# A decoder layer on one core: the last job's inverse sums spread by TensorE, VectorE's steps reordered, maxima in two operations per block

## The reference, cut to what matters

```python
# x (4, 1024, 256), 16 heads of 16; ctx (4, 77, 256)
x = x + attn(layernorm(x))            # windowed causal self attention, chunks of 128, each with the chunk before
x = x + xattn(layernorm(x), ctx, ctx) # cross attention on 77 keys with a mask
x = x + ffn(layernorm(x))             # fake-quantised gated feed-forward, 704 wide
...
def xattn(...):
    attn = softmax(scores)            # per head and token
    out = einsum('bhqk,bhkd->bhqd', attn, v)
    return out @ Wo.T + bo
...
def ffn(x, ...):
    xq = act_fake_quant(x, clip_x)    # scale = sigmoid(clip) * max|x| / 127 over the WHOLE tensor
    h = act_fake_quant(silu(xq @ Wg.T) * (xq @ Wu.T), clip_down)   # again one scale from max|h| over everything
    return h @ Wd.T                   # weights fake-quantised per row
```

## Time and profile before

| | us |
|---|---|
| median of 3 runs | 696.22 |
| lowest and highest | 692.82, 696.35 |
| profiled execution, time | 694.38 |
| its span, first to last instruction | 692.5 |
| busy: TensorE, VectorE, ScalarE, GpSimd | 606.5, 513.6, 406.5, 165.0 |
| passage, last value product to the first quantised x | 552 to 582 |
| up phase | 587 to 651 |
| down phase, to the end | 655 to 692.5 |

### The profile page before, as it was taken

How to read it: one execution, slowest core, us unless ns; L and a number is a source line. 1 busy time by engine, 2 the same in 40 slices (tenths; PEclk the granted TensorE clock), 3 DMA queues, 4 the chain that set the end, 5 groups by cost and what they waited for, 6 DMA issues and landing times.

```text
span 692.5 us, 19989 instructions
## 1 busy us (share of the span) xinstructions
PE 606.5 (88%) x8020; PEld 394.3 (57%) x8020; DVE 513.6 (74%) x986; ACT 406.5 (59%) x602; POOL 165.0 (24%) x213
## 2 busy tenths in 40 slices
PE   2799999999998999999999999999979843887395
PEld 2567575767764766576757655567546532333173
DVE  6698777777787586757866866686697466799787
ACT  3346666665675548556564576444545714999692
POOL 2014333322343302320441133220120001455200
PEclk9899999999999999999999999999999966999789
DMA  7744233552353344256324353443474320000024
GB/s 255 189 152 132 58 119 98 153 147 77 99 144 102 109 114 103 70 147 158 113 73 128 90 131 103 112 121 85 99 212 102 76 48 1 0 1 1 0 92 153
DMA packets 58554, 72.17 MB, mean 104 GB/s; under 512 B 23979, under 2 KB 35423, under 8 KB 58463
## 3 DMA queue, kind: packets, MB, share of 16 engines
q1 hardware_dynamic: 54783, 68.92, 35.9%
q10 hardware_dynamic: 3680, 1.97, 1.1%
HBM read 17.74 MB, written 4.72 MB: 32 GB/s over the span
## 4 chain that ended last, share of the span: by engine, by line
PE 57%; DVE 14%; SPq 10%; DMA 6%; issue 6%; ACT 4%; POOL 0%; ACTq 0%; DVEq 0%; POOLq 0%
PE banks L483 37%; PE banks L663 7%; SPq L416 5%; PE banks L583 4%; PE banks L674 3%; DVE mtop L1100 3%; SPq L434 2%; SPq L411 2%; PE banks L527 2%; DVE tops L1283 2%; PE banks L728 1%; DVE big L1277 1%; DMA oTs<-oe 1%; DVE parts L1265 1%; DMA big<-parts 1%
## 5 line engine op out<-in xcount | busy, mean ns | idle before, releaser
L483 PE MATMUL banks<-big 96*128 96x77 bf16 (+3 forms) x1344 | 157.6, 238 | 9.3 <-DMA big<-kparts 2.9
L1100 DVE TENSOR_REDUCE mtop<-banks 128x4 f32<-128x640 f32 (+3 forms) x128 | 127.2, 1020 | 40.6 <-PE banks L592 39.8
L483 PEld LDWEIGHTS banks<-big 99*128 99x128 bf16 (+2 forms) x1344 | 102.2, 101 | 75.7 <-issue 34.8
L899 ACT ACTIVATE big<-banks 128x1024 f32<-128x1024 f32 x96 | 97.0, 1028 | 38.3 <-PE banks L483 38.0
L1380 POOL TENSOR_SCALAR_AFFINE_SELECT big<-big 128x512 f32<-128x512 f32 x96 | 64.5, 672 | 229.8 <-ACT big L899 228.9
L483 PE MATMUL banks<-xnT,weights 128*128 128x512 f32 x192 | 91.6, 606 | 0.1
L583 PE MATMUL banks<-big 96*32 96x160 bf16 (+3 forms) x1792 | 71.3, 259 | 0.5 <-DVE mtop L1100 0.2
L903 ACT ACTIVATE big<-banks 77x1024 f32<-77x1024 f32 x48 | 47.9, 1021 | 27.4 <-PE banks L483 25.4
L1104 DVE TENSOR_REDUCE mtop<-banks 128x8 f32<-128x616 f32 x64 | 49.3, 790 | 17.5 <-PE banks L483 17.2
L663 PE MATMUL banks<-big 128*17 128x256 f32 x768 | 57.0, 382 | 0.0
L912 ACT COPY oe<-banks 128x512 f32<-128x512 f32 x64 | 36.7, 588 | 33.6 <-DMA oTx<-oe 10.7
(11 more groups left out here) (160 smaller groups left out, 1187.0 us busy)
## 6 DMA issues: line engine op xcount, KB each, us to landing
big<-parts SPq DMA_DIRECT2D x285, 128.0 KB, 2.4
oc<-sums SPq DMA_DIRECT2D x16, 512.0 KB, 4.7
oTs<-oe SPq DMA_DIRECT2D x64, 64.0 KB, 2.5
...
```

The costliest lines, as they stand in the source:

```text
L483: return e.matmul(to[0:w], k[:, 0:w], q, start=start, stop=stop, skip_group_check=True)
L899: e.activation(pt[u].rearrange("p (i n) -> p i n", i=4)[:, :, 0:n], pair(p).rearrange("p j (s n) -> p (j s) n", s=2)[:, :, 0:n], ACT.Exp, ...
L1100: e.tensor_reduce(M.rearrange("p (h c) -> p h c", h=4)[:, :, c], pair(p).rearrange("p j (s n) -> p (j s) n", s=2)[:, :, 0:160 + 32 * (c % 4)],
```

## The change

Four things change.

- The last job's inverse sums (x31) don't go through DRAM. Its store and widen are gone. GpSimd builds a 128x128 matrix of ones and zeros (`heads`: row p has ones in the 16 columns of its head) in the step pick, in the middle of the kernel, and VectorE a 128x16 one (`group`). In the new steps broad, VectorE multiplies the 128x64 reciprocals by `group` into a 128x512 operand for each half of the tokens, and TensorE multiplies it by `heads`, which gives each partition its head's inverse sums, in a PSUM bank. The scaling of x31 reads that bank in place of `oc`. The two new bank holders shift the banks of the four last out steps and of the last wturn.
- On VectorE, the steps stat3 2 5, 2 6 and 2 7, top3 2 4 and 2 6, root3 2, and wtile 1 4, 1 5, 2 0 and 2 1 stand ahead of the last invert. Before, they stood between it and the scaling of x31, or behind that (wtile 2 1). Then follow invert x31, broad 0, broad 1, scale x30, scale x31 and end3 2. On SyncE, the spreads of x31's second group stand directly behind its gather.
- On TensorE the two broad products stand between the wturn 2 0 and the first out step of x3.
- In the up phase the tops of a block are two operations of three tiles, put behind tiles 1 and 4 of the next block, in place of three of two tiles behind tiles 0, 2 and 5. Block 7 keeps three of two tiles. So there are 17 maxima in place of 24.

```diff
--- before.py
+++ after.py
@@ -27,6 +27,7 @@
 JOBS = [(j[0].lower(), int(j[1]), "ab".index(j[2]))
         for j in "S0a S0b S1a S1b S2a X0a S2b X0b S3a X1a S3b X1b X2a X2b X3a X3b".split()]
 AT = {j: n for n, j in enumerate(JOBS)}
+LAST_SELF = [j for j in JOBS if j[0] == "s"][-1]
 UNITS = {"s": NC, "x": 4}
 HALF_AT = {"s": 3, "x": 1}
 
@@ -41,9 +42,9 @@
     "sgvmrTqpsvmtvexmvmqsccosmdosmvmemvsmssvhvrmmtwomsnipvsmvemhmgsqnhscvrqhmmAqsvnvsCogeccxsvqvnBvtcpsou"
     "rsVosvDMuedpVMtsvmnvegnvmsyknosmysvvmmsmemivmwsnRrqNvecqmAvBocptsvmmsmvmssmmveesTyNmrvvsgTysvsyitqqs"
     "veCskxdvvssvmwmvycgsemspvACcsmvgvpsmvstsvveBrkyhmvvmemxsysgsrsdptvimvmmwuvemevrqqCgYussAsmvsmvxvmccd"
-    "vtehmeoonnonipsnrsonnhntsnBsRwhvmmmveANvgpCmgNBssTsevTrxqqccpodwtomoUgosmyvvuvvemmkeshysprtys1svmykv"
-    "gimmquysvsveesmhrCcsvvutveuvAhdmxyqesycs2mysmYmpsvvhwitgvrveh22km3B4mmsmxses4r44v4o45t4oy4o5y5osp4mv"
-    "554memmeryiUuvvu5styysspsiv5yeyxuvvye5Y5vg5sssseue44vU4vvxvd455p5ogyyowgjyyojdypyojyyJYjJJJ6E5w")
+    "vtehmeoonnonipsnrsonnhntsnBsRwhvmmmveANvgpCmgNBssTsevTrxqqccpodwtomoUgosmyvvuvvemmkeshysprtysP1svmyk"
+    "vgimmquysvsveesmhrCcsvvutveuvAhdmxyqesycs2mysmYmpsvvhwitgvrveh22km3B4mmsmxses4r44v4o45t4oy4o5y5osp4m"
+    "v554memmeryiUuvvu5styysspsv5yeyuvvye5Y5vg5sssseue44v4vvvd455p5ibbxxUogyyowgjyyojypyojyyJYjJJJ6E5")
 
 
 def root_of(kind, b, c):
@@ -70,8 +71,10 @@
         "g": [("gather", job, g) for job, g in turns],
         "p": [("spread", job, g) for job, g in turns],
         "i": [("invert", job) for job in JOBS],
-        "d": [("store", job) for job in JOBS],
-        "w": [("widen", job) for job in JOBS],
+        "d": [("store", job) for job in JOBS[:-1]],
+        "w": [("widen", job) for job in JOBS[:-1]],
+        "b": [("broad", half) for half in range(2)],
+        "P": [("pick",)],
         "x": [("scale", job) for job in JOBS],
         "o": [("out",) + layer + (c,) for layer in layers for c in range(0, NC, 2)],
         "n": [("stats",) + layer + (c,) for layer in layers for c in range(NC)],
@@ -130,7 +133,7 @@
 
 
 WIDE = {"turned": 2, "max": 2, "score": 2, "up": 2}
-NARROW = {"turnw", "turnc", "masks", "keys", "qk", "v", "xkeys", "turnm", "out", "wturn", "turnx", "down", "dsc", "peak"}
+NARROW = {"turnw", "turnc", "masks", "keys", "qk", "v", "xkeys", "turnm", "out", "broad", "wturn", "turnx", "down", "dsc", "peak"}
 
 
 def banks_of(steps, count_of):
@@ -217,6 +220,9 @@
         winv = sb("winv", [128, 16], F32)
         banks = ctx.enter_context(nc.psum_tensor("banks", [128, 8, 512], F32))
         acc = banks[:, 6:8, :]
+        heads = big[:, 21888:22016]
+        group = big[:, 22016:22032]
+        grown = rem.rearrange("p i n -> p (i n)")
         r_dram = nc.dram_tensor("sums", [8, S], F32, kind="Internal").ap()
 
         x_dram = x_in.rearrange("b (c p) d -> p (b c) d", p=128)
...
@@ -317,6 +324,8 @@
                 return a_xnT, 2 * n
             if k == "wturn":
                 return a_wT, w_done(s)
+            if k == "broad":
+                return d_scale, len(JOBS) + s[1]
             return {"turnw": a_turnw, "turnc": d_ctx, "masks": d_mask, "keys": a_keys, "qk": d_rem, "v": a_v,
                     "xkeys": d_xv, "max": d_max, "turnm": a_m3t, "score": a_exp, "out": d_out}[k], {
                         "turnw": 2 * n, "masks": 2 * n, "keys": 3 * n - 2, "xkeys": 2 * n}.get(k, n)
@@ -685,6 +694,10 @@
                             t = whole(bank(p)[:, i * 256:i * 256 + 256], oT[kind][f][:, (c + i) * 128:(c + i) * 128 + 128],
                                        wo[:, f, :] if kind == "s" else xw[:, 3, f, :], i == 0 and f == 0, f == 1)
                     t.then_inc(t_out, 1)
+                elif k == "broad":
+                    e.wait_ge(p_pick, 3)
+                    e.wait_ge(d_broad, s[1] + 1)
+                    whole(bank(p), heads, grown[:, s[1] * 512:s[1] * 512 + 512], True, True).then_inc(t_broad, 1)
                 elif k == "wturn":
                     _, z, t0 = s
                     e.wait_ge(a_wb, n_of["wtile", z, t0])
@@ -775,11 +788,11 @@
                 if blk < 6 and t in (1, 3):
                     ffn += [("narrow", blk + 2, t - 1), ("narrow", blk + 2, t)]
                 ffn.append(("hid", blk, t))
-                if blk and t in (0, 2, 5):
-                    ffn.append(("top", blk - 1, t // 2 * 2))
+                if blk and t in (1, 4):
+                    ffn.append(("top", blk - 1, 0 if t == 1 else 3, 3))
                 if blk == 7 and t in (3, 5):
-                    ffn.append(("top", 7, t - 3))
-        ffn += [("top", 7, 4), ("scaleh",), ("peak", 1), ("quanth", 0), ("dsc",)]
+                    ffn.append(("top", 7, t - 3, 2))
+        ffn += [("top", 7, 4, 2), ("scaleh",), ("peak", 1), ("quanth", 0), ("dsc",)]
         for blk in range(8):
             if blk < 7:
                 ffn.append(("quanth", blk + 1))
@@ -1124,16 +1137,37 @@
                     if n:
                         e.wait_ge(land_r, 32 * n - 16)
                     e.reciprocal(ls[:, 1, :], ls[:, 0, :]).then_inc(d_inv, 1)
+                elif k == "pick":
+                    e.wait_ge(p_set, 2)
+                    e.wait_ge(t_val, n_of[end_val(LAST_SELF, 1)])
+                    e.tensor_reduce(group, ident.rearrange("p (h j) -> p j h", h=8), AX.X, ALU.max).then_inc(d_pick, 1)
+                elif k == "broad":
+                    e.wait_ge(d_inv, len(JOBS))
+                    if s[1] == 0:
+                        e.wait_ge(d_pick, 1)
+                        e.wait_ge(a_p1, n_of["split", JOBS[-1], 0, 1])
+                        e.wait_ge(d_p2, n_of["split", JOBS[-1], 0, 1])
+                    e.tensor_tensor(grown[:, s[1] * 512:s[1] * 512 + 512].rearrange("p (j n) -> p j n", j=8),
+                                    ls[:, 1, :].rearrange("p (a n) -> p a n", a=1).to_broadcast([128, 8, 64]),
+                                    group[:, 8 * s[1]:8 * s[1] + 8].rearrange("p (j a) -> p j a", a=1
+                                                                              ).to_broadcast([128, 8, 64]),
+                                    ALU.mult).then_inc(d_broad, 1)
                 elif k == "scale":
                     job = s[1]
                     kind, b, f = job
                     n = AT[job]
-                    e.wait_ge(land_r, 32 * (n + 1))
+                    last = n == len(JOBS) - 1
+                    if not last:
+                        e.wait_ge(land_r, 32 * (n + 1))
                     for g in range(2):
                         e.wait_ge(land_o[g], 64 * (n + 1))
-                    cuts = (0, 512, S) if n == len(JOBS) - 1 else (0, S)
-                    for a, z in zip(cuts, cuts[1:]):
-                        e.tensor_tensor(oT[kind][f][:, a:z], oT[kind][f][:, a:z], oc[:, a:z], ALU.mult).then_inc(d_scale, 1)
+                    if last:
+                        for half in range(2):
+                            to = oT[kind][f][:, half * 512:half * 512 + 512]
+                            e.wait_ge(t_broad, half + 1)
+                            e.tensor_tensor(to, to, bank(at_bank["broad", half][0]), ALU.mult).then_inc(d_scale, 1)
+                    else:
+                        e.tensor_tensor(oT[kind][f], oT[kind][f], oc[:, :], ALU.mult).then_inc(d_scale, 1)
                 elif k == "out":
                     _, kind, b, c = s
                     t0 = NC * b + c
@@ -1277,16 +1311,16 @@
                     e.scalar_tensor_tensor(hb[:, t0, blk * 512:blk * 512 + 512], bank(p, 1), winv[:, 6 + t0:7 + t0],
                                            sgb[:, i:i + 512], ALU.mult, ALU.mult).then_inc(f_hd, 1)
                 elif k == "top":
-                    _, blk, t0 = s
-                    e.wait_ge(f_hd, 3 * blk + t0 // 2 + 1)
-                    e.wait_ge(f_hp, 3 * blk + t0 // 2 + 1)
-                    e.tensor_reduce(tops[:, blk * 3 + t0 // 2:blk * 3 + t0 // 2 + 1],
-                                    hb[:, t0:t0 + 2, blk * 512:blk * 512 + 512], AX.XY, ALU.max, apply_absolute_value=True
+                    _, blk, t0, n = s
+                    e.wait_ge(f_hd, 3 * blk + (t0 + n + 1) // 2)
+                    e.wait_ge(f_hp, 3 * blk + (t0 + n) // 2)
+                    e.tensor_reduce(tops[:, f_n[s] - 1:f_n[s]],
+                                    hb[:, t0:t0 + n, blk * 512:blk * 512 + 512], AX.XY, ALU.max, apply_absolute_value=True
                                     ).then_inc(f_top, 1)
                 elif k == "scaleh":
-                    e.wait_ge(f_top, 24)
-                    e.tensor_reduce(amx[:, 4:5], tops[:], AX.X, ALU.max).then_inc(f_top, 1)
-                    e.wait_ge(f_top, 25)
+                    e.wait_ge(f_top, 17)
+                    e.tensor_reduce(amx[:, 4:5], tops[:, 0:17], AX.X, ALU.max).then_inc(f_top, 1)
+                    e.wait_ge(f_top, 18)
                     e.wait_ge(f_hp, 24)
                     scales(amx[:, 4:5], 1, 7)
```

(10 more changed lines are left out.)

11 lines of the change are left out of this document (6 added, 5 removed).

## The result

| | before | after |
|---|---|---|
| median of 15 runs, us | 694.92 | 689.22 |
| lowest | 692.82 | 686.15 |
| ratio of the times | | 0.9909 (0.9889 to 0.9930) |
| span of the profiled execution | 692.5 | 686.2 |
| last value product ends | 552.1 | 553.6 |

The change makes the kernel 6.3 us faster (4.9 to 7.7). One of the 15 runs of the changed kernel took 2068.5 us; nothing here explains it, and the ratio doesn't rest on it.

What follows compares the result with a forecast made beforehand. The prediction took the last job's DMA round, then VectorE, to bound the passage, and VectorE the up phase, ScalarE just behind. From the median 696.22 it took 5.8 and 0.9, 6.7 together, giving 689.5 us, range 685.5 to 694.

Steps and rivals of the forecast that it cites:

- The passage: Stretch from attention to the feed-forward part, 550 to 582 us; forecast 5.8 us shorter, bounds 4.4 to 7.
- the return of the clock: In the passage, TensorE's high clock was to return 3.3 to 5.3 us after the broad products start at 557.0.
- the DMA round: End of attention: x31's inverse sums no longer stored and widened by DMA; part of the first output step's 3.65 us gain.
- the open steps: VectorE's 5.9 us of steps not needing x31's sums, moved into its 4.97 us wait; reciprocal 0.9 us later.
- The helper step pick: Near 490 us, GpSimd builds a matrix and VectorE reduces it; costed at nothing, 0.2 us without the idle cover.
- The up phase: Some 590 to 651 us; forecast 0.9 us shorter, VectorE's period 7.4 us a block, bounds -4 to +2.5.
- the floor: In the up phase, with both narrow pairs free VectorE needs 6.6 us a block and ScalarE bounds with 7.1.
- The first (a clock that holds): Rival: high clock holds in the passage and both narrow pairs run free; about 686.5 us, chance 0.12.
- The third (both pairs meet): Rival: in the up phase both narrow pairs meet GpSimd's products, period 8.4; about 694.3 us, chance 0.10.
- the fourth (three locks): Rival: each of a block's three GpSimd products holds VectorE fully, 10.4 us a block; 704 us, chance 0.03.
- The fifth: Rival: spreads or broadcast products come late in the passage; at 4 us late 693.5 us, chance 0.04.
- The second: Rival: clock stays low through the outputs until about 569, passage gains 2 us; 693.3 us, chance 0.10.

Runs made afterwards that it cites:

- passage_only: The changed kernel with the old tops, three of two tiles per block; ratio 0.9918 to the kernel before, 5.7 us under it.
- top3_behind: The changed kernel with top3 2 6 moved on VectorE from ahead of the last reciprocal to behind the scaling of x31; ratio 0.9886 to the kernel before.
- clock_up: The changed kernel with idle matmuls (results unread) on TensorE in the gaps ahead of the feed-forward part; ratio 0.9844 to the kernel before.
- narrow_together: The changed kernel with all four narrow steps of a block behind hid 0, not two each behind hid 0 and hid 2; ratio 0.9895 to the kernel before.
- reorder_only: The kernel before with VectorE's open steps ahead of the last reciprocal, the sums still going by DMA; ratio 1.0022.
- products_early: The changed kernel with VectorE in the old order and TensorE's broad products ahead of the transposes of weight tiles 1 4 to 2 0; ratio 0.9982 to before.
- before_clock: The kernel before with 40 idle matmuls (results unread) on TensorE in the passage; ratio 0.9928, 5.0 us under before.
- clock_passage: The changed kernel with eight idle matmuls (results unread) in TensorE's gap ahead of the transpose of weight tile 1 4; ratio 0.9868 to the kernel before.
- clock_all: The changed kernel with the idle matmuls of clock_passage and clock_up and 34 more around the second maximum; ratio 0.9782 to the kernel before, median 681.4 us.

## Why the prediction was right, point by point

**The passage.** Forecast 5.8 us, measured in this trace 7.1. Step by step, all in us behind the last value product:

| | forecast | after | the other four kernels with this passage |
|---|---|---|---|
| reciprocal | 3.6 | 3.3 | 2.7 to 3.3 |
| broad on VectorE, both | 1.30 | 1.29 | 1.29 |
| first broad product | 4.9 | 4.7 | 4.1 to 4.7 |
| scaling of x31 begins | 6.8 | 6.9 | |
| first output step | 8.5 | 7.7 | 7.6 to 8.3 |
| first addition | 10.9 | 9.7 | 10.2 to 10.7 |
| passage | 24.2 | 22.9 | 23.1 to 23.9 |

(The four are passage_only, top3_behind, clock_up and narrow_together.) The order of events is that of the forecast, and so is the reason why no wait is left ahead of the second output. The term that was mis-sized is the return of the clock. The forecast took 3.3 to 5.3 us from the start of the products; the five traces show 2.3, 4.0, 4.3, 4.5 and 5.0. The trace of the changed kernel had the shortest, and that was luck: the other four gained 6.1 to 6.9 us in place of 7.1. The bounds of 4.4 to 7 us for the passage are missed by 0.1. The five passages spread over 1.0 us, which is the spread that the prediction gave them.

**What made the gain.** The prediction named two things, the DMA round that goes and the open steps that fill VectorE's wait. It didn't say that neither is worth anything alone. reorder_only (1.0022) and products_early (0.9982) show it. The clock was an entry in the sum; before_clock and clock_passage give it a size of some 2.1 of 7.1 us.

**The helper step pick.** Costed at nothing. In its trace VectorE's reduction took 0.35 us and stood ahead of 2.6 us of idle time, where the earlier trace rows has 2.89.

**The up phase.** Forecast 0.9, measured 1.2. The forecast's own terms, 0.15 us on five blocks and 0.3 at the end, make 1.05 and not 0.9; measured are 0.85 on blocks 1 to 5 and 0.29 in block 7. The top of three tiles was forecast with 1.65 to 1.72 us and takes 1.66 by the distance of the starts. The merge is worth nothing, as said: 2 x 1.66 against 3 x 1.12. The second pair meets GpSimd and the first doesn't, as said. The period was forecast to fall from 7.56 to 7.4. In the traces it isn't one number: over blocks 1 to 5 it runs from 7.70 to 7.55 before (mean 7.61) and from 7.56 down to 7.33 after (mean 7.44), as the meeting costs less from block to block (the second pair takes 1.68, then 1.57, then 1.47 us). Here is a detail of the lock that the prediction left out: GpSimd's product at 602.93 takes 1.48 us where 1.27 is usual, because the narrow step began 0.05 us earlier. This is the rule of the Trainium skill, "SBUF — State Buffer", section "SBUF: two separate sides", that whichever of the two starts first gets the shared ports for its whole instruction and the other waits. The trace agrees in both directions: a pair of 0.72 us takes 1.57 when GpSimd was first (610.42 behind 610.26), and GpSimd's product 1.48 when VectorE was. narrow_together removed the lock and found ScalarE behind it, which the prediction had as the floor, but at 7.37 and not 7.1: ScalarE's silu of tile 5 waits for products that wait for hid 2.

**Own time and median.** The forecast of 689.5 took the median as its base and was met by 689.22. Part of that is luck: the forecast took 6.7 off 696.22, the median of three runs, but the median of 15 is 694.92, and the measured gain is 5.7 between the medians and 6.3 by the ratio. The traces save 7.1 and 1.2 us, 8.3 together, or 7.7 with the mean of the five passages (23.5), and the spans differ by 6.3. The rest is lost elsewhere: 1.5 us in attention, whose last value product ends at 553.6 in place of 552.1, and 0.5 in the down phase. The prediction had neither.

The traces show what happened in attention, and it is the clock again. At 210 us TensorE waits for a DMA. In the trace of the kernel before it waited 1.84 us and kept the high level; in that of the changed kernel it waited 2.53, the granted clock fell at 212.4 and came back at 215.9, and a step of VectorE that both kernels have, 0.1 us ahead at 208 us, was 1.9 us behind at 247. Before:

```profile
211.99 0.31 PE L483 MATMUL banks<-big 96*128 96x77 bf16 x4 [1.84 <-DMA big<-kparts]
...
246.81 0.42 DVE L1046 BATCH_NORM_STATS2 st<-xs 128x6 f32<-128x256 f32 x1
```

After, with the stretch in which the level changes back:

```profile
212.60 0.42 PE L492 MATMUL banks<-big 96*128 96x77 bf16 x4 [2.53 <-DMA big<-kparts]
...
248.68 0.42 DVE L1059 BATCH_NORM_STATS2 st<-xs 128x6 f32<-128x256 f32 x1
...
214.00:216.00 2.00, 2.00 (x18) 1.75 (x16) 1.37 (x3) 1.02 (x1) 0.16 (x1) 0.54 0.60 201
```

Five of the 14 traces have this fall, after waits of 1.95 to 2.53 us, and need 40.2 to 40.6 us between those two steps of VectorE. The nine others waited 1.23 to 2.11 us and need 38.1 to 38.9. A second fall, between 515 and 531 us, stands in eight traces, for 3.4 to 10.2 us. From TensorE's restart at about 513 us, behind a wait of 1.4 us, to the last value product these eight need 39.5 to 41.1 us, the other six 38.6 to 39.6. The four traces without the broad steps end attention at 551.6 to 554.0 us, and only the latest of them (reorder_only) has such a fall; the ten with them end it at 553.6 to 557.2, and each has one or both. The first fall lies ahead of every step that the change touches, and in reorder_only the second lies ahead of every step in which it differs from the kernel before. Whether the change makes such falls more frequent or the traces drew them by chance is not shown, nor what they do to the medians. That the prediction came so close to the median owes something to this: a passage better than forecast and an attention part that was later.

**The rivals.** The first (a clock that holds) did not happen but was made: clock_passage. The third (both pairs meet) and the fourth (three locks) did not occur in any of the 14 traces: no block has more than one pair over 0.8 us. The fifth did not either: SyncE issued the spreads from 554.97 to 557.4, and VectorE's scaling waited for TensorE alone. The second was there in a mild form, with the clock back up to 5.0 us after the products' start.

**Open.** Whether the change brings on the falls of the clock in attention; the 0.6 us in clock_all; the 2 us of before_clock beyond its passage; and the single run of 2068 us. None was tried.
